# Reading the group and slot numbers for four visits at once in two edge sums of a GNN kernel

## The chip, the core and the metric

The kernel runs on one core of one Trainium2 chip. The metric is the device time in microseconds of one execution of the whole program.

## The reference, cut to what matters

The program computes four graph layers one after the other on one graph of 6,250 nodes and 100,000 edges, sorted by target node: two GAT convolutions, a GCN layer, a relational attention layer and a GGN (gated) layer, with a residual and a layer norm behind each. The change touches the edge sums of the GCN and of the GGN layer. What these must compute is a weighted and a plain sum of source rows by target node:

```
msgs = xw[row] * norm[:, None]                                   # GCN
out  = jax.ops.segment_sum(msgs, col, num_segments=n)
agg  = jax.ops.segment_sum(m[src], dst, num_segments=n_nodes)    # GGN
```

A row has 128 float32 numbers. Nodes are kept in 49 blocks of 128.

## The kernel before, in words

**Groups and visits.** The edges are cut into 196 groups (`GROUPS`) of 512 edges (`GE`), each as four tiles (`GT`) of 128 edges, one edge to a partition. A group touches one block of target nodes or, at a border, two or more. A pair of a group and a block is a visit; there are 244 (`V`). A visit multiplies, for each of the four tiles, a one-hot matrix (edge against node of the block, 128x128) with the gathered rows (128x128) on TensorE and adds the four products up in PSUM. Which group, which block and which buffer slot a visit has is only known at run time; an earlier stage writes these numbers into rows in SBUF (`grp_row`, `blk_row`, `slot_row`), and `done_row` says for each group which visit is its last.

**Who does what, in both stages.** All loops are written out in the program; nothing branches.

- POOL (`gather_rows`, L256) gathers the rows of each group with four indirect DMAs into one of 14 slots (`SLOTS`). From the fifteenth group on it first reads `done_row` (L956) and waits on `s_used`, which is the counter `s_o` of TensorE's finished visits, until the last visit of the group that held the slot is done.
- SP (`announce`, L965) waits for the four gathers of a group and adds one to `s_landed`.
- DVE makes the one-hot of the next visit (`front`, four operations, L1864 or L2051; two buffers), waits for TensorE's finished visit `s_o`, and adds the PSUM result to the accumulator (`back`, L1872 or L2059). It counts `s_oh` and `s_acc`.
- TensorE, per visit: it reads the group number (`group_of`, L975) and the slot number (`slot_of`, L978) from SBUF into registers, waits for the one-hot (`s_oh`), for the group's rows (`s_landed`) and for the accumulation of the visit two back (`s_acc`), and issues four float32 matmuls (L1946 in GGN, L2116 in GCN), whose last adds one to `s_o`. In the trace one such matmul is two weight loads and two matmul records.
- In the GCN stage TensorE has a second job after each of the first 208 visits (`static`, L2127): four small bf16 matmuls that pick node values for a later layer. It reads the four block numbers for it in one instruction (`several`, L969). ACT and DVE serve this job too (L2015, L2071, L2072), and ACT stores the one-hots it made to memory.

**Order.** Each engine runs its own program in order and meets the others only at semaphores. POOL may be up to 14 groups ahead of the last finished visit. A visit's number reads stand in TensorE's program behind the matmuls of the visit before.

**Around it.** The GCN stage begins with POOL's and TensorE's first instruction together. In the GGN stage POOL gathers its first 14 groups while TensorE and ACT do another job (13 rounds of four transposes and two matmuls, L1923 to L1936); visits start after it. What follows each stage waits for all of it.

Of the kernel before, what the change touches and what calls it, by code (L numbers as in the profile page):

```python
# [32 lines left out]
D = 128  # L33
# [9 lines left out]
V = GROUPS + BLOCKS - 1  # L43
# [7 lines left out]
RING = 4  # L51
# [37 lines left out]
def build(nc, A, out):  # L89
    top = ExitStack()  # L90
    with top:
# [885 lines left out]
        def slot_of(eng, v):  # L977
            return eng.value_load(slot_row[0:1, bass.ds(v, 1)], min_val=0, max_val=SLOTS - 1)  # L978

# [846 lines left out]
        def ggn_edges():  # L1826

            with phase() as st:
# [18 lines left out]
                with nc.Block() as block:  # L1847
# [69 lines left out]
                    def _(pe):  # L1917
# [19 lines left out]
                        for i in range(0, V // RING):  # L1937
                            for k in range(RING):
                                v = i * RING + k
                                g = group_of(pe, v)  # L1940
                                slot = slot_of(pe, v)
                                pe.wait_ge(s_oh, v + 1)
                                pe.wait_ge(s_landed, g + 1)
                                pe.wait_ge(s_acc, v + 1)
                                for t in range(GT):
                                    m = nc.tensor.matmul(ps_o[k % 2][:, 0:D], oh[:, k % 2, t, :], rows[:, bass.ds(slot, 1), t, :].rearrange("p o d -> p (o d)"),  # L1946
                                                         start=(t == 0), stop=(t == GT - 1))
                                m.then_inc(s_o, 1)


        def gcn_edges():
            with phase() as st:
# [33 lines left out]
                with nc.Block() as block:  # L1986
# [117 lines left out]
                    def _(pe):  # L2104
# [4 lines left out]
                        def body(n, k):  # L2109
                            g = group_of(pe, n)  # L2110
                            slot = slot_of(pe, n)
                            pe.wait_ge(s_oh, n + 1)
                            pe.wait_ge(s_landed, g + 1)
                            pe.wait_ge(s_acc, n + 1)
                            for t in range(GT):
                                m = mm(ps_o[k % 2][:, 0:D], oh[:, k % 2, t, :], rows[:, bass.ds(slot, 1), t, :].rearrange("p o d -> p (o d)"),  # L2116
                                       start=(t == 0), stop=(t == GT - 1))
# [13 lines left out]
                        for k in range(RING):  # L2131
                            body(k, k)
                            static(0, k)
                        for i in range(1, ITERS // RING):
                            for k in range(RING):
                                body(i * RING + k, k)
                                static(i, k)
                        for n in range(ITERS, V):
                            body(n, n % RING)
# [658 lines left out]
```

## Time and profile before

| what | us |
|---|---|
| median of 3 executions (lowest, highest) | 7929.77 (7909.9, 7938.46) |
| span of the profiled execution (the page gives no time of its own for it) | 7961.8 |
| GCN edge stage, first to last visit | 3380 to 4611 |
| GGN edge stage, first to last visit | 6761 to 7861 |
| PE busy, share of the span | 3988.6, 50% |
| DVE busy | 3552.5, 45% |
| POOL busy | 4190.2, 53% |

PE is TensorE's array, PEld its weight loads, PEldq and the other names with q an engine's own instruction queue: reads of numbers, register arithmetic and waits, which don't count as busy. In a row of the timeline the last bracket is the idle time of the engine before the row and what ended it; "issue" is time in which the engine waited for nothing that the profile shows. A releaser is inferred, and can be named after a line that is long over. The clock column is the granted TensorE clock as a share of full speed: 0.5 is 1.2 GHz, 1.0 is 2.4 GHz.

### The profile page before, as it was taken

The page shows a single profiled execution, that of the slowest core. Times are in us where ns is not written, and L with a number is a line of the kernel's source. Part 1 is how long each engine was busy: PE and PEld are TensorE (multiplying, and loading weights), DVE is VectorE, ACT ScalarE, POOL GpSimd, SP SyncE. Part 2 cuts the span into 40 slices and gives each one's busy share as a digit, 9 for nine tenths or more (in the row PEclk, how much of TensorE's full clock was granted, in tenths as well). Part 3 has the DMA queues.
Part 4 walks back from the last instruction along what each step waited for, and adds up shares of the span by engine and source line. Part 5 has one row for each costly group of instructions (what it writes and reads, how often), then busy time and mean ns, then how long its engine had stood idle before and what let it go on. Part 6 is the DMA issues. An engine that isn't in the chain of part 4 may idle for free. (4 is left out here: it accounts for less than half of the span.)

```text
span 7961.8 us, 106930 instructions
## 1 busy us (share of the span) xinstructions
PE 3988.6 (50%) x29332; PEld 3225.4 (41%) x29332; DVE 3552.5 (45%) x10985; ACT 1543.9 (19%) x3920; POOL 4190.2 (53%) x4416
## 2 busy tenths in 40 slices
PE   2401645540164442334444458888888585333446
PEld 1301534530154432323444446666666473233334
DVE  3002965530297442423333355555555693122224
ACT  0001730010174000200000033444344213000003
POOL 6474035537503566466665635555555644666662
PEclk8655557775555766655555578888888797566568
DMA  5233445643344554345666424445444372111111
GB/s 147 75 105 96 146 125 171 188 117 106 94 145 131 161 168 140 108 104 141 149 150 147 109 87 143 147 149 149 145 147 145 79 206 64 46 46 45 45 45 32
DMA packets 564740, 944.43 MB, mean 119 GB/s; under 512 B 122022, under 2 KB 226111, under 8 KB 563599
## 3 DMA queue, kind: packets, MB, share of 16 engines
q1 hardware_dynamic: 263779, 403.40, 15.9%
q0 software_dynamic: 140576, 316.92, 15.5%
q10 hardware_dynamic: 159840, 217.27, 9.7%
q8 instruction: 290, 4.75, 0.3%
q14 instruction: 255, 2.09, 0.1%
HBM read 703.64 MB, written 235.53 MB: 118 GB/s over the span
## 5 line engine op out<-in xcount | busy, mean ns | idle before, releaser
L256 POOL DMA_INDIRECT s_rows<-rel_tab,src_v x832 | 813.4, 978 | 700.0 <-DVE s_msg L2489 424.7
L256 POOL DMA_INDIRECT stash<-gat_tab,src_g x784 | 790.9, 1009 | 724.5 <-POOLq L111 383.2
L256 POOL DMA_INDIRECT stash<-in_x,src_g x736 | 740.4, 1006 | 719.3 <-POOLq L111 382.6
L1163 PE MATMUL g_psc<-g_parts,g_oh 128*128 128x52 bf16 x9408 | 507.0, 220 | 1060.3 <-issue 796.5
L256 POOL DMA_INDIRECT gcn_rows<-gcn_tab,src_g x784 | 753.0, 960 | 461.8 <-issue 222.4
L256 POOL DMA_INDIRECT ggn_rows<-ggn_tab,src_g x784 | 744.2, 949 | 423.0 <-issue 231.0
L1600 PE MATMUL e_psb<-tmp,e_oh 128*128 x3328 | 565.5, 334 | 751.4 <-DVE e_oh L1571 470.4
L1163 PEld LDWEIGHTS g_psc<-g_parts,g_oh 128*128 128x128 bf16 x9408 | 439.7, 120 | 1128.2 <-issue 843.8
L1600 PEld LDWEIGHTS e_psb<-tmp,e_oh 128*128 128x128 f32 x3328 | 510.5, 237 | 806.7 <-issue 806.5
L1946 PE MATMUL ggn_pso<-ggn_rows,ggn_oh 128*128 x1952 | 448.7, 390 | 652.3 <-issue 277.2
L2116 PE MATMUL gcn_pso<-gcn_rows,gcn_oh 128*128 x1952 | 503.3, 433 | 531.4 <-issue 387.1
L1946 PEld LDWEIGHTS ggn_pso<-ggn_rows,ggn_oh 128*128 128x128 f32 x1952 | 371.1, 277 | 730.5 <-issue 729.8
L2116 PEld LDWEIGHTS gcn_pso<-gcn_rows,gcn_oh 128*128 128x128 f32 x1952 | 425.0, 317 | 566.2 <-issue 564.8
L1095 DVE TENSOR_TENSOR g_eq<-g_eq,g_psc 128x416 f32<-128x416 f32 x392 | 227.6, 581 | 832.3 <-remote 572.0
L1055 ACT ACTIVATE acc<-g_lo_rows,g_neg_pid 128x512 f32<-128x512 bf16 x392 | 283.0, 722 | 1008.7 <-issue 776.1
L1872 DVE TENSOR_TENSOR acc<-acc,ggn_pso 128x128 f32 x244 | 69.8, 286 | 915.7 <-DMA edge_v<-acc 626.2
L2059 DVE TENSOR_TENSOR acc<-acc,gcn_pso 128x128 f32 x244 | 69.8, 286 | 784.1 <-remote 517.2
L1569 DVE COPY tmp<-gx 128x12 f32<-128x12 f32 x392 | 75.7, 193 | 680.5 <-DMA edge_v<-stash 288.4
L2558 PE MATMUL s_psk<-w_kv,s_msgT 128*128 128x128 f32 x1664 | 301.0, 336 | 0.0
L1571 DVE TENSOR_TENSOR e_oh<-iota,drel_v 128x512 f32<-128x512 f32 x416 | 284.3, 683 | 21.7 <-PE e_psb L1600 21.7
L2563 PE MATMUL s_psv<-w_kv,s_msgT 128*128 128x128 f32 x1664 | 280.8, 325 | 0.2
L2558 PEld LDWEIGHTS s_psk<-w_kv,s_msgT 128*128 128x128 f32 x1664 | 254.2, 234 | 58.1 <-issue 58.1
(503 smaller groups left out, 8232.0 us busy)
## 6 DMA issues: line engine op xcount, KB each, us to landing
edge_v<-stash SPq DMA_DIRECT2D x392, 256.0 KB, 2.1
g_lo_rows<-lo_rows ACTq DMA_DIRECT2D x392, 256.0 KB
e_values<-edge_v SPq DMA_DIRECT2D x392, 256.0 KB
oh_dram<-tmp ACTq DMA_DIRECT2D x208, 256.0 KB
s_oh<-oh_dram SPq DMA_DIRECT2D x208, 256.0 KB
edge_v<-acc SPq DMA_DIRECT2D x208, 256.0 KB
r_values<-edge_v SPq DMA_DIRECT2D x208, 256.0 KB, 3.0
tmp<-drel_rows ACTq DMA_DIRECT2D x208, 128.0 KB
```

The lines of the kernel that those rows point to most:

```text
L256: pool.indirect_dma_start(rows[:, t, :], None, tab[:, :], bass.IndirectOffsetOnAxis(ap=edges[:, t:t + 1], axis=0)).then_inc(s_land, 16)
L1055: nc.scalar.activation(sq[:, k % 2, :], trow[:, k, GE:2 * GE], ACT.Square, bias=neg_pid[:, :]).then_inc(s_sq, 1)
L1095: v.tensor_tensor(eq[:, k % 2, :, :, :], eq[:, k % 2, :, :, :], cand, ALU.mult).then_inc(s_take, 1)
L1163: m = nc.tensor.matmul(ps_c[k % 2][:, a * GT + t, 0:NBP], oh[:, k, a * GE + t * P:a * GE + (t + 1) * P], part[:, a, n, :], start=(n == 0), ...
L1569: v.tensor_copy(wv4[:, k, :, D:WCOLS], w.rearrange("p h t -> p t h"))
L1571: v.tensor_tensor(oh[:, k % RING, :, :], iota[:, :].unsqueeze(1).to_broadcast([P, GT, P]), drel_v[:, bass.ds(n * GT, GT)].unsqueeze(2).to_ ...
L1600: nc.tensor.matmul(ps_b[:, bass.ds(bank, 1), 0:WCOLS].rearrange("p o d -> p (o d)"), oh[:, k, t, :], wv[:, bass.ds(slot, 1), :].rearrange( ...
L1872: v_.tensor_tensor(ab, ab, ps_o[k % 2][:, 0:D], ALU.add).then_inc(s_acc, 1)
L1946: m = nc.tensor.matmul(ps_o[k % 2][:, 0:D], oh[:, k % 2, t, :], rows[:, bass.ds(slot, 1), t, :].rearrange("p o d -> p (o d)"), start=(t == ...
L2116: m = mm(ps_o[k % 2][:, 0:D], oh[:, k % 2, t, :], rows[:, bass.ds(slot, 1), t, :].rearrange("p o d -> p (o d)"), start=(t == 0), stop=(t = ...
L2558: m = mm(ps_k[:, t, :], msgT[:, T[t]], w_kv[:, 0, :], start=False, stop=(t == GT - 1))
L2563: m = mm(ps_v[:, t, :], msgT[:, T[t]], w_kv[:, 1, :], start=True, stop=True)
```

## The change

TensorE no longer reads two numbers for each visit. At the first of every four visits (`RING` is 4) it reads the group number of the fourth of them, reads the four slot numbers with one instruction, and waits until the rows of the fourth visit's group have landed. The three visits behind it have no number reads and no wait on `s_landed`. The waits on `s_oh` and `s_acc`, the matmuls and all other engines' programs stay as they were. In GCN the second job stays between the visits; its loop is rewritten so that the visits 208 to 243 run through the same code.

```diff
-                                g = group_of(pe, v)
-                                slot = slot_of(pe, v)
+                                if k == 0:
+                                    newest = group_of(pe, v + RING - 1)
+                                    slots = several(mybir.EngineType.PE, slot_row[0:1, bass.ds(v, RING)], SLOTS - 1)
+                                    pe.wait_ge(s_landed, newest + 1)
                                 pe.wait_ge(s_oh, v + 1)
-                                pe.wait_ge(s_landed, g + 1)
                                 pe.wait_ge(s_acc, v + 1)
                                 for t in range(GT):
-                                    m = nc.tensor.matmul(ps_o[k % 2][:, 0:D], oh[:, k % 2, t, :], rows[:, bass.ds(slot, 1), t, :].rearrange("p o d -> p (o d)"),
+                                    m = nc.tensor.matmul(ps_o[k % 2][:, 0:D], oh[:, k % 2, t, :], rows[:, bass.ds(slots[k], 1), t, :].rearrange("p o d -> p (o d)"),
                                                          start=(t == 0), stop=(t == GT - 1))
                                 m.then_inc(s_o, 1)
...
-                        def body(n, k):
-                            g = group_of(pe, n)
-                            slot = slot_of(pe, n)
+                        def numbers(n):
+                            newest = group_of(pe, n + RING - 1)
+                            slots = several(mybir.EngineType.PE, slot_row[0:1, bass.ds(n, RING)], SLOTS - 1)
+                            pe.wait_ge(s_landed, newest + 1)
+                            return slots
+
+                        def body(n, k, slots):
                             pe.wait_ge(s_oh, n + 1)
-                            pe.wait_ge(s_landed, g + 1)
                             pe.wait_ge(s_acc, n + 1)
...
-                        for k in range(RING):
-                            body(k, k)
-                            static(0, k)
-                        for i in range(1, ITERS // RING):
+                        for i in range(0, V // RING):
+                            slots = numbers(i * RING)
                             for k in range(RING):
-                                body(i * RING + k, k)
-                                static(i, k)
-                        for n in range(ITERS, V):
-                            body(n, n % RING)
+                                body(i * RING + k, k, slots)
+                                if i < ITERS // RING:
+                                    static(i, k)
```

`several`, which both versions have, reads a row of numbers into as many registers with one instruction.

## Rows read from the trace of the kernel before

**Rows 1.** Stretches of both stages: us, busy by engine (count), clock, DMA share, GB/s.

```profile
3380.00:4611.00 1231.00, 553.90 (x2784) 485.33 (x2784) 447.72 (x1642) 39.74 (x210) 745.57 (x777) 0.52 0.52 130
4578.00:4611.00 33.00, 24.00 (x128) 20.66 (x128) 20.01 (x77) 0.00 (x0) 0.00 (x0) 0.80 0.00 1
6761.00:7861.00 1100.00, 448.31 (x1952) 370.93 (x1952) 269.26 (x1224) 0.04 (x1) 691.30 (x728) 0.62 0.17 44
7829.00:7861.00 32.00, 23.11 (x129) 19.82 (x128) 16.46 (x76) 0.00 (x0) 0.00 (x0) 0.82 0.00 1
```

**Rows 2.** Groups of the GCN stage: busy us, mean ns | idle before, releasers.

```profile
L256 POOL DMA_INDIRECT gcn_rows<-gcn_tab,src_g x777 | 745.6, 960 | 449.4 <-issue 220.5 <-remote 115.5 <-PE gcn_pso L2116 113.4
L2116 PE MATMUL gcn_pso<-gcn_rows,gcn_oh 128*128 x1952 | 503.3, 433 | 531.4 <-issue 387.1 <-DVE acc L2059 97.5 <-DVE gcn_oh L2051 25.1
```

**Rows 3.** The same groups of the GGN stage.

```profile
L256 POOL DMA_INDIRECT ggn_rows<-ggn_tab,src_g x728 | 691.3, 950 | 396.5 <-issue 204.5 <-DMA edge_v<-acc 145.4 <-PE ggn_pso L1946 46.6
L1946 PE MATMUL ggn_pso<-ggn_rows,ggn_oh 128*128 x1952 | 448.7, 390 | 652.3 <-issue 277.2 <-DVE acc L1872 262.8 <-DVE ggn_oh L1864 103.8
L1872 DVE TENSOR_TENSOR acc<-acc,ggn_pso 128x128 f32 x243 | 69.5, 286 | 914.0 <-DMA edge_v<-acc 626.2 <-PE ggn_pso L1946 228.6 <-issue 59.1
```

**Rows 4.** Timeline after the last gather, GGN: start us, us, what [idle before, releaser].

```profile
7835.52 0.97 PEld L1946 LDWEIGHTS ggn_pso<-ggn_rows,ggn_oh 128*128 128x128 f32 x8 [0.85 <-issue]
7835.52 1.15 PE L1946 MATMUL ggn_pso<-ggn_rows,ggn_oh 128*128 x8 [0.67 <-DVE acc L1872]
7836.89 0.29 DVE L1872 TENSOR_TENSOR acc<-acc,ggn_pso 128x128 f32 x1 [0.75 <-PE ggn_pso L1946]
7837.10 0.87 DVE L1864 TENSOR_SCALAR ggn_oh<-iota,dst_tab 128x128 f32<-128x128 f32 x4
7837.55 0.97 PEld L1946 LDWEIGHTS ggn_pso<-ggn_rows,ggn_oh 128*128 128x128 f32 x8 [1.07 <-issue]
```

**Rows 5.** Timeline after the last gather, GCN, weight loads at half clock.

```profile
4578.69 1.78 PEld L2116 LDWEIGHTS gcn_pso<-gcn_rows,gcn_oh 128*128 128x128 f32 x8 [1.07 <-issue]
4580.72 1.78 PEld L2116 LDWEIGHTS gcn_pso<-gcn_rows,gcn_oh 128*128 128x128 f32 x8 [0.24 <-issue]
```

**Rows 6.** Slot read L978 after the last gather: ns min/median/max.

```profile
L978 PEldq TENSOR_LOAD <-slot_row x15: 299/300/307, 7830.5 to 7859.1; - x15
L978 PEldq FUSED_REGOPS  x16: 151/151/151, 7828.9 to 7859.5; - x16
L978 PEldq SEQ_ASSERT  x16: 18/18/18, 7829.1 to 7859.7; - x16
```

**Rows 7.** Slot read L978 at 6770.5 to 6784 us, gathers running.

```profile
L978 PEldq FUSED_REGOPS  x2: 697/703/709, 6772.0 to 6782.5; - x2
```

**Rows 8.** Four-number read in the GCN stage.

```profile
L969 PEldq TENSOR_LOAD <-blkv_row x208: 5/342/934, 3380.4 to 4502.9; - x104
```

**Rows 9.** Timeline of the first waits of POOL and one round, GGN.

```profile
6762.85 0.94 POOL L256 DMA_INDIRECT ggn_rows<-ggn_tab,src_g  x1 [24.54 <-PE ggn_pso L1946]
6791.81 0.94 POOL L256 DMA_INDIRECT ggn_rows<-ggn_tab,src_g  x1 [3.10 <-DMA edge_v<-acc]
6796.74 0.97 PEld L1946 LDWEIGHTS ggn_pso<-ggn_rows,ggn_oh 128*128 128x128 f32 x8 [0.33 <-issue]
6806.13 0.29 DVE L1872 TENSOR_TENSOR acc<-acc,ggn_pso 128x128 f32 x1 [8.24 <-DMA edge_v<-acc]
6820.57 0.29 DVE L1872 TENSOR_TENSOR acc<-acc,ggn_pso 128x128 f32 x1 [13.38 <-DMA edge_v<-acc]
6820.75 0.94 POOL L256 DMA_INDIRECT ggn_rows<-ggn_tab,src_g  x1 [4.20 <-DMA edge_v<-acc]
```

**Rows 10.** Stretches of the GGN opening, with gathers and without.

```profile
6694.00:6737.00 43.00, 9.61 (x16) 3.53 (x15) 0.00 (x0) 3.94 (x6) 32.64 (x35) 0.50 0.20 54
6750.00:6759.00 9.00, 9.00 (x29) 4.71 (x27) 0.00 (x0) 6.93 (x11) 0.00 (x0) 0.89 0.01 2
```

**Rows 11.** Landing announcements L965, GCN.

```profile
L965 SPq EVENT_SEMAPHORE  x195: 17/17/17, 3384.2 to 4577.9; - x195
```

More of the change, by code:

```diff
@@ L975, in group_of @@
             return eng.value_load(grp_row[0:1, bass.ds(v, 1)], min_val=0, max_val=GROUPS - 1)
-        def slot_of(eng, v):
-            return eng.value_load(slot_row[0:1, bass.ds(v, 1)], min_val=0, max_val=SLOTS - 1)
         def landed(name, slots=SLOTS):
@@ L2107, in _ @@
                         pe.sem_inc(s_acc, 2)
-                        def body(n, k):
-                            g = group_of(pe, n)
-                            slot = slot_of(pe, n)
+                        def numbers(n):
[4 more added lines that the diff above has]
+                        def body(n, k, slots):
                             pe.wait_ge(s_oh, n + 1)
-                            pe.wait_ge(s_landed, g + 1)
                             pe.wait_ge(s_acc, n + 1)
                             for t in range(GT):
-                                m = mm(ps_o[k % 2][:, 0:D], oh[:, k % 2, t, :], rows[:, bass.ds(slot, 1), t, :].rearrange("p o d -> p (o d)"),
+                                m = mm(ps_o[k % 2][:, 0:D], oh[:, k % 2, t, :], rows[:, bass.ds(slots[k], 1), t, :].rearrange("p o d -> p (o d)"),
                                        start=(t == 0), stop=(t == GT - 1))
```

## The prediction

> **What bounds the kernel now.** I first took the busy times by stretch, for the two stages that the change touches. GCN takes 1231 us and GGN 1100 us [rows 1]. In neither is an engine full: PE's array is busy for 554 and 448 us, DVE for 448 and 269, POOL for 746 and 691. The groups of instructions say more. POOL's gathers take 0.96 and 0.95 us each, and between two of them stand some 0.3 us of "issue", which no other engine causes: 745.6 + 220.5 = 966 us in GCN and 691.3 + 204.5 = 896 us in GGN [rows 2, 3]. The remainder of POOL's idle time is waiting, 115.5 + 113.4 = 229 us in GCN, and 145.4 + 46.6 = 192 us in GGN, of which 24.5 us is the first wait, before any visit is done [rows 2, 3, 9]. The rest, 229 + 167.5 = 396 us, are waits for a slot, so for finished visits of TensorE. After the last landing each stage still runs for 33 and 32 us [rows 1, 11]: some 16 visits that TensorE is behind. So the path through a stage is POOL's gathers, its waits for TensorE, and the visits left over at the end.
>
> Why is TensorE behind? With the gathers over, a visit takes 2.03 us from start to start, and it takes the same 2.03 us whether its eight weight loads take 0.97 us (full clock) or 1.78 us (half clock) [rows 4, 5]. The array is not what bounds it, and DVE's 0.29 + 0.87 us isn't either [rows 4]. What is left is the queue of instructions: a number read is 0.30 us of load, 0.15 us of clamp and 0.02 us of assertion [rows 6], with gaps some 0.65 us, and there are two in a row for each visit. At 2.03 us, 244 visits would need 495 us, under half of either stage, and TensorE would never be behind. But while the gathers run it falls into another gait. In the round of [rows 9] POOL resumes at 6791.81; the visit that starts at 6796.74 should end 1.15 us later, as in [rows 4], and DVE takes its result only at 6806.13, where 0.22 us after the end is the rule with the gathers over. The next result is taken at 6820.57, and then POOL resumes after a wait of 4.2 us. At the same time single instructions of TensorE's queue, which take 0.15 us undisturbed, take 0.7 us [rows 6, 7]. So TensorE's reports of finished work arrive late while POOL gathers, its queue crawls, and POOL runs out of slots because of it. DVE's idle 626 us in GGN is the same thing seen from DVE (the releaser's name there is a line long over) [rows 3].
>
> **What the change removes.** Per four visits, eight reads of three queue instructions each become one such read and one four-number read, which the same engine does in 0.34 us in the GCN stage [rows 8]: 8 x 0.65 = 5.2 us of queue time become 0.65 + 0.40 = 1.05 us. Counted in instructions, a GGN visit has 12 in the queue (two reads of three, two waits or sums, four address computations) and 16 array instructions, 28 in all. Afterwards it has 5 and a quarter of 6, so 6.5, and 22.5 in all. With the second job a GCN visit goes from 47 to 41.5. Nothing is moved on SP, POOL, ACT or DVE, and no DMA is touched.
>
> *The end of each stage.* Here it counts in full. Without the reads the queue needs 2.03 - 1.3 + 0.26 = 1.0 us for a visit, and the next bound takes over: over two visits, a visit's matmuls 1.15, the way to DVE 0.22, 0.21 until its one-hots start and 0.87 for them, then TensorE again [rows 4], (1.15 + 0.22 + 0.21 + 0.87)/2 = 1.2 us and a little for issue, at full clock; 1.8 us at half clock by the weight loads [rows 5]. The clock is 0.8 there [rows 1], and I take 1.6 us. 16 visits x 0.43 = 7 us in each stage, **14 us** (bounds: 4 us if all ran at half clock, 2 x 16 x 0.8 = 26 us at full clock).
>
> *POOL's waits.* How much of the 396 us goes depends on what makes the reports late, which no row shows. The least is nothing, if the queue's instructions have no part in it. The most by this count is that the waits vanish. In between: if the late reports are a backlog to which each instruction of TensorE adds alike, a round carries more visits in the proportion of the counts, and the waits shrink by 5.5/28 = 20% in GGN and 5.5/47 = 12% in GCN: 33 + 27 = **60 us**. I take this value. It is near the lower end, since most of what TensorE does, the array's 16 or 24 instructions, stays.
>
> *The new wait.* Behind it stand the block's four visits, and with them DVE's additions, ACT's copies and POOL's slots. As long as TensorE is some 14 groups behind POOL, the fourth visit's rows have long landed and it costs nothing. At the head of the GCN stage they have not: a group lands every 5 us (four gathers of 1.25), the second at 3384.2 [rows 11], so the fourth at about 3394, and the first visit starts 14 us later. POOL has slots until its fifteenth group, 70 us in, so only part of it comes through: between 0 and 14 us, I take **3 us**. In GGN all 14 groups are there before the first visit.
>
> **The sum.** -14 - 60 + 3 = -71 us. The durations are from an execution with a span of 7961.8 us, 32 us or 0.4% above the median; the difference is put on the median: 7929.8 - 71 = **7859 us**.
>
> The Trainium skill, in "NOTIFIC — the notification-queue block", section on the write path and its measured rates, says that an instruction's own record costs an engine no cycles, though the block's inner queue can hold its producers back when it is full. By the first half the reads that are gone never cost more than their 0.65 us, and the sum would be 7929.8 - 14 + 3 = 7919 us. The trace speaks against it: 0.7 us for an instruction of 0.15 us [rows 6, 7]; no row shows that it is records which are held back.
>
> **The rivals.**
>
> *The waits stay* (7919 us, no change). The backlog comes from the array's instructions alone. For it: in the opening of the GGN stage TensorE's program has no number reads and hardly any waits, and yet with the gathers running PE is busy for 9.6 of 43 us, against 9.0 of 9.0 us once they pause [rows 10]. The late reports need no number reads. Then only the stage ends gain: 7929.8 - 14 + 3 = 7919.
>
> *The crawl goes by the queue.* In it each of a visit's queue steps costs 0.7 us [rows 7], 12 and four matmuls today, 6.5 and four afterwards. The visits in a crawl would come in 10.5/16 of the time, and about half of GGN's and a quarter of GCN's waits would go: 84 + 57 + 14 - 3 = 152 us, 7778 us. Against it: DVE waits for a report, not for a queue, in the long gaps of [rows 9].
>
> *The crawl is gone altogether.* It came from number reads and gathers together. All 396 us go, and TensorE follows POOL so closely that only the last four visits are left after the last landing, 6 instead of 33 us twice: 7929.8 - 396 - 53 = 7481 us. Against it stand again [rows 10].
>
> *Slower: denser visits fill the backlog sooner.* If what TensorE may leave unreported is used up in a fixed time or by the rate of its matmuls, then visits at 1.4 to 1.8 us after each resumption of POOL, instead of 2.03, start the crawl earlier, and their four-visit heads, which wait for both reads and rows, fall into it. Of about five visits that a GGN round carries (from 6791.81 to the wait before 6820.75 are 24.7 us, 20 gathers, so five groups), half a one would be lost, so 10% more rounds and waits: +40 us. With the whole 14 us at the head of GCN and the end's gain: 40 + 14 - 14 = +40 us, 7970 us. It decides from the point where a round carries fewer than the present visits. For it: POOL resumes at 6791.81 and the visit of 6796.74, five microseconds on, is already late [rows 9].
>
> That the change does not do what it says is not likely: the four-number read is in use in the same stage [rows 8].
>
> **How the numbers follow.** A measurement of this kernel can tell about 0.5%, or 40 us, from no change. The forecast has 0.40, on its own from 7810 to 7900; most of it is beyond 40 us. The waits that stay have 0.24, the queue's crawl 0.17, its end 0.08, the slower case 0.11. Faster by over 0.5%: 0.38 + 0.17 + 0.08 + a little of the second case, 0.65. Within 0.5%: 0.26. Slower: 0.09, as the slower case lies at its border. The range goes from 7740 to 7960: below it lies the vanished crawl, above it half of the slower case.
>
> **What would show each step.** (1) After the last gather, visits in both stages at 1.3 to 1.8 us instead of 2.03; if they stay at 2.03, the queue was not the bound. (2) POOL's waits, without the first: 134 us in GGN and 202 us in GCN; 168 and 229 if the array alone makes the backlog, near nothing if the crawl is gone. (3) Undisturbed reads of the group number 61 times in each stage, the four-number read of the slots 61 times at about 0.34 us. (4) The first GCN visit at about 3394 instead of 3380. (5) All other stages as before. The forecast is wrong if POOL's waits grow, or if they fall by more than half.

## The result

The changed kernel takes 7866.8 us (median of 20 runs; the kernel before beside it 7934.1 us, of 20 runs). The ratio is 0.9928 with a 95% interval of 0.9909 to 0.9947, so 57 us less (42 to 72). The medians differ by 67 us: three of the changed kernel's 20 runs had a granted clock of 0.56 to 0.58 instead of 0.67 and took 7949 to 7963 us, and the ratio leaves out only the longest of them, as a slow run. A later measurement gave 0.9934 (0.9912 to 0.9955). The prediction was 7859 us, between 7740 and 7960: the direction and the size are right. On one chip, though (chip B below), where both kernels run in 6000 us, the same change made the kernel slower by 0.25%. The experiments below show what is missing on that chip, and most likely why the change costs time there.

### The profile page after: what moved, and what is told of

The parts are those of the page before. It is cut to its first block and busy times, and to the rows that moved or that the text cites. A ratio compares the mean times of both kernels' runs of the same rounds, so it can differ in the third digit from the quotient of the medians.

```text
span 7853.1 us, 104124 instructions
## 1 busy us (share of the span) xinstructions
PE 3880.8 (49%) x29332; PEld 3174.1 (40%) x29332; DVE 3549.2 (45%) x10985; ACT 1546.6 (20%) x3920; POOL 4220.9 (54%) x4416
## 3 DMA queue, kind: packets, MB, share of 16 engines
q8 instruction: 279, 4.57, 0.2%
## 5 line engine op out<-in xcount | busy, mean ns | idle before, releaser
L256 POOL DMA_INDIRECT s_rows<-rel_tab,src_v x832 | 818.7, 984 | 685.7 <-DVE s_msg L2487 411.6
L256 POOL DMA_INDIRECT gcn_rows<-gcn_tab,src_g x784 | 756.7, 965 | 418.2 <-issue 225.8
L256 POOL DMA_INDIRECT ggn_rows<-ggn_tab,src_g x784 | 746.7, 952 | 411.6 <-issue 234.3
L1597 PE MATMUL e_psb<-tmp,e_oh 128*128 x3328 | 584.8, 341 | 708.2 <-DVE e_oh L1568 379.8
L1597 PEld LDWEIGHTS e_psb<-tmp,e_oh 128*128 128x128 f32 x3328 | 527.9, 244 | 765.4 <-issue 765.0
L1944 PE MATMUL ggn_pso<-ggn_rows,ggn_oh 128*128 x1952 | 381.6, 368 | 704.4 <-DVE ggn_oh L1861 302.4
L1944 PEld LDWEIGHTS ggn_pso<-ggn_rows,ggn_oh 128*128 128x128 f32 x1952 | 344.4, 269 | 742.3 <-issue 740.5
L2117 PE MATMUL gcn_pso<-gcn_rows,gcn_oh 128*128 x1952 | 444.5, 402 | 159.7 <-issue 118.3
L2117 PEld LDWEIGHTS gcn_pso<-gcn_rows,gcn_oh 128*128 128x128 f32 x1952 | 387.4, 295 | 178.2 <-issue 173.2
L2128 PE MATMUL pre_psr<-vt_nv_pieces,tmp 128*128 x832 | 92.9, 181 | 526.5 <-DVE tmp L2070 348.7
L2128 PEld LDWEIGHTS pre_psr<-vt_nv_pieces,tmp 128*128 128x128 bf16 x832 | 81.2, 113 | 565.9 <-issue 551.3
```

Of the source, the lines that this page charges most:

```text
L256: pool.indirect_dma_start(rows[:, t, :], None, tab[:, :], bass.IndirectOffsetOnAxis(ap=edges[:, t:t + 1], axis=0)).then_inc(s_land, 16)
L1597: nc.tensor.matmul(ps_b[:, bass.ds(bank, 1), 0:WCOLS].rearrange("p o d -> p (o d)"), oh[:, k, t, :], wv[:, bass.ds(slot, 1), :].rearrange( ...
L2128: m = mm(ps_n[k % 2][:, t, :], oh2[:, k, t * P:(t + 1) * P], nvp[:, bass.ds(b, 1), :].rearrange("p o n -> p (o n)"), start=True, stop=True)
```

## The profile after

The stretches of both stages and their ends, to be read against [rows 1] (us, then busy time and count of PE, weight loads, DVE, ACT and POOL; granted clock, DMA share, GB/s):

```profile
3343.00:4534.00 1191.00, 511.09 (x2784) 453.34 (x2784) 446.37 (x1657) 39.96 (x210) 756.72 (x784) 0.58 0.52 136
4508.00:4534.00 26.00, 20.60 (x139) 17.70 (x138) 21.12 (x84) 0.00 (x0) 0.67 (x1) 0.95 0.06 6
6575.00:7753.00 1178.00, 423.11 (x2051) 362.75 (x2049) 276.68 (x1234) 24.71 (x39) 746.32 (x784) 0.62 0.17 44
7724.00:7753.00 29.00, 21.55 (x144) 19.81 (x144) 19.32 (x92) 0.00 (x0) 0.42 (x1) 0.85 0.04 6
```

These windows reach from the first gather to the last addition, those of [rows 1] from the first visit. Measured from first gather to last addition in both traces, GCN went from 1240.5 to 1190.9 us and GGN from 1192.9 to 1178.2: 49.6 and 14.7 us, 64 in all. The two profiled spans differ by 109 us (7961.8 and 7853.1). The other 45 us lie in stages that the change doesn't touch: the span before is 28 us above the median of 7934.1, the span after 14 us below its own.

POOL, DVE and PE in the two stages, against [rows 2, 3] (busy us, mean ns | idle us before, releasers):

```profile
L256 POOL DMA_INDIRECT gcn_rows<-gcn_tab,src_g x784 | 756.7, 965 | 418.2 <-issue 225.8 <-remote 157.9 <-PE gcn_pso L2117 25.2
...
L2117 PE MATMUL gcn_pso<-gcn_rows,gcn_oh 128*128 x1952 | 444.5, 402 | 159.7 <-issue 118.3 <-DVE gcn_oh L2049 22.3 <-DVE acc L2057 12.4
...
L256 POOL DMA_INDIRECT ggn_rows<-ggn_tab,src_g x784 | 746.7, 952 | 411.6 <-issue 234.3 <-DMA edge_v<-acc 133.6 <-PE ggn_pso L1944 43.6
...
L1869 DVE TENSOR_TENSOR acc<-acc,ggn_pso 128x128 f32 x244 | 70.0, 287 | 901.1 <-DMA edge_v<-acc 667.0 <-PE ggn_pso L1944 208.8 <-issue 25.0
...
L1944 PE MATMUL ggn_pso<-ggn_rows,ggn_oh 128*128 x1952 | 381.6, 368 | 704.4 <-DVE ggn_oh L1861 302.4 <-issue 277.4 <-DVE acc L1869 123.9
```

A gather still takes 0.95 to 0.97 us and its issue 0.3 us. What is left of POOL's idle time is waiting for slots: 418.2 - 225.8 = 192 us in GCN, where it was 229, and 411.6 - 234.3 - 24.3 (the first wait) = 153 us in GGN, where it was 167.5. DVE's idle time before its additions in GGN is 901 us where [rows 3] has 914 (the row after also includes the first addition, which in the trace before adds under 2 us), so the late reports are nearly all still there.

After the last gather, two visits of GGN and the start of the next two, against [rows 4] (start us, us, what [idle before, releaser]):

```profile
7737.06 2.12 PE L1944 MATMUL ggn_pso<-ggn_rows,ggn_oh 128*128 x16 [0.58 <-DVE acc L1869]
7738.51 0.29 DVE L1869 TENSOR_TENSOR acc<-acc,ggn_pso 128x128 f32 x1 [0.73 <-PE ggn_pso L1944]
7738.71 0.87 DVE L1861 TENSOR_SCALAR ggn_oh<-iota,dst_tab 128x128 f32<-128x128 f32 x4
7739.49 0.28 DVE L1869 TENSOR_TENSOR acc<-acc,ggn_pso 128x128 f32 x1
...
7739.72 2.13 PE L1944 MATMUL ggn_pso<-ggn_rows,ggn_oh 128*128 x16 [0.54 <-DVE ggn_oh L1861]
```

Two visits now take 7739.72 - 7737.06 = 2.66 us, 1.33 each, and TensorE waits for one-hots and additions and no longer for its queue.

A round of GGN with the gathers running, against [rows 9]: POOL's resumption, DVE's additions, POOL's next resumption:

```profile
6772.57 0.95 POOL L256 DMA_INDIRECT ggn_rows<-ggn_tab,src_g  x1 [4.69 <-DMA edge_v<-acc]
...
6781.23 0.29 DVE L1869 TENSOR_TENSOR acc<-acc,ggn_pso 128x128 f32 x1 [2.90 <-PE ggn_pso L1944]
...
6794.64 0.29 DVE L1869 TENSOR_TENSOR acc<-acc,ggn_pso 128x128 f32 x1 [12.21 <-DMA edge_v<-acc]
...
6806.55 0.29 DVE L1869 TENSOR_TENSOR acc<-acc,ggn_pso 128x128 f32 x1 [10.84 <-DMA edge_v<-acc]
...
6807.12 0.94 POOL L256 DMA_INDIRECT ggn_rows<-ggn_tab,src_g  x1 [4.73 <-DMA edge_v<-acc]
```

The long gaps are still there. But from 6772.57 to the wait before 6807.12 are 29.8 us, 24 gathers, six groups, where the round of [rows 9] has five. These are single rounds. Over the whole GGN stage, from one gap between gathers of over 3 us to the next, POOL now gathers 5.9 groups in the mean instead of 5.1; the gaps of over 1 us are 48 instead of 53, and about as long as before (3.4 for 3.3 us in the mean).

The reads in GGN: the group numbers now come 61 times, the four slots in one load:

```profile
L975 PEldq TENSOR_LOAD <-grp_row x61: 302/305/314, 6665.4 to 7746.5; - x61
...
L969 PEldq TENSOR_LOAD <-slot_row x61: 328/332/334, 6666.1 to 7747.1; - x61
```

No load is slowed here, gathers or not. The clamps show the same. Before, of the slot number with the gathers running (ns min/median/max), then after, of the group number over the whole stage:

```profile
L978 PEldq FUSED_REGOPS  x227: 2/151/715, 6762.3 to 7825.2; - x114
...
L975 PEldq FUSED_REGOPS  x61: 151/151/157, 6665.8 to 7746.8; - x61
```

With the gathers running, 296 of 1815 steps of register arithmetic and assertion in TensorE's GGN queue took over 0.5 us before the change, and none of 1015 does after it; in GCN it was 228 of 2645 and is 19 of 1854. The slow queue that [rows 7] shows is gone from GGN and nearly gone from GCN. The reports are no earlier for it: from a visit's last matmul to DVE's addition it took 2.9 us in the mean in GCN and 5.2 us in GGN, and it takes 5.3 and 5.9 us now.

## The experiments

In what follows a *pause* is a gap of over 1 us between two gathers, less the 0.3 us of issue; a *report's delay* is the time from a visit's last matmul to DVE's addition. Both are worked out from the events of a trace. Four of the runs fell on one chip (A), four on a second (B), four on a third (C); the changed kernel ran again on B and C. The chip of the first measurement, that of the result and of the profiles before and after, isn't on record. The kernel before was profiled only there, so its pauses and stages are known only from it. The edits are shortened; those of "the wait without the reads" and "each read twice" are against the kernel before, the others against the changed kernel.

**The reads without the wait.** Four group numbers are read at once too, and each visit waits for its own group:

```diff
-newest = group_of(pe, v + RING - 1)
+groups = several_checked(PE, grp_row[0:1, bass.ds(v, RING)], GROUPS - 1)
 slots = several(PE, slot_row[0:1, bass.ds(v, RING)], SLOTS - 1)
-pe.wait_ge(s_landed, newest + 1)
 pe.wait_ge(s_oh, v + 1)
+pe.wait_ge(s_landed, groups[k] + 1)
```

> The changed kernel, but TensorE also reads the four group numbers at once, and each visit waits for the rows of its own group, as before the change. So it has the fewer reads without the new wait. Compare with the changed kernel (7866.8 us; POOL's waits of over 1 us: 165.1 us in GCN, 162.7 in GGN; a visit every 1.49 and 1.42 us after the last gather; first GCN visit 21.8 us after the first gather). If the gain is the reads' alone (my theory): first GCN visit back to some 9.5 us after the first gather, all else as in the changed kernel, time 7855 to 7870 us. If the wait at the head of four was what helped (it lets a backlog drain, a rival): POOL's waits back towards 210 and 174 us, time 7900 us or more.

Measured on A: 8007.4 us beside 8041.2 of the kernel before, ratio 0.9956 (0.9938 to 0.9973). The first GCN visit is back at 10.8 us after the first gather. But pauses are 189 and 182 us, and the ratio isn't that of the changed kernel. Its checked read brings instructions of its own: it has 1708 fewer than the kernel before, 3.5 for each of the 488 visits, where the change has 5.75 fewer. So a gain is there without the wait, 35 us of it. That the rest is missing because fewer instructions are saved is an argument; this run alone would also allow the wait a share, which the next one has to tell.

**The wait without the reads.** Both reads of each visit stay; the first of four reads the fourth's group and waits for it, the other three don't wait for rows:

```diff
-g = group_of(pe, v)
+g = group_of(pe, v + RING - 1 if k == 0 else v)
 slot = slot_of(pe, v)
 pe.wait_ge(s_oh, v + 1)
-pe.wait_ge(s_landed, g + 1)
+if k == 0:
+    pe.wait_ge(s_landed, g + 1)
```

> The kernel before with its two reads for each visit, but the first visit of four reads the group number of the fourth and waits for it, and the other three wait for no rows. The new wait alone. If it costs only at the head of GCN (my theory): first GCN visit some 22 us after the first gather instead of 9.5, POOL's waits as before (210 and 174 us of pauses over 1 us, within 15), visits after the last gather 2.06 us, time 0 to 14 us over the kernel before. If the wait is part of the gain (rival): POOL's waits fall by over 20 us and the time is 7900 us or less. If it costs in every block of four: POOL's waits grow by over 20 us.

Measured on A: 8033.6 us, ratio 0.9989 (0.9976 to 1.0001), pauses 201 and 180 us, first GCN visit at 22.2 us. Its pauses and its visits at the stage ends (1.97 us) are about those of the profile before (210 and 174, 2.06). The new wait is not the gain (9 us at most likely, between -1 and 19) nor, on this chip, a loss that can be seen.

**Each read twice.** Six queue instructions more for each visit than before the change:

```diff
+group_of(pe, v)
+slot_of(pe, v)
 g = group_of(pe, v)
 slot = slot_of(pe, v)
```

> The kernel before with each of the two number reads of a visit done twice: 6 instructions more in TensorE's queue per visit, the change the other way round. If every TensorE instruction adds alike to the backlog (my forecast's term): POOL's waits grow by 6/28 in GGN and 6/47 in GCN (+37 and +27 us), and the visits after the last gather go from 2.06 to some 3.3 us (+40 us in both stages): 8030 us. If only the array's instructions make the backlog: waits as before, only the visits at the stage ends slower: about 7970 us. If the crawl goes by queue instructions at 0.7 us each: 6 x 0.7 us more for every visit that runs in it, waits grow by 38% (+145 us): 8120 us or more.

Measured on A: 8362.1 us, ratio 1.0408 (1.0384 to 1.0433), 321 us more than the kernel before (328 by the ratio). The rows of POOL:

```profile
L256 POOL DMA_INDIRECT gcn_rows<-gcn_tab,src_g x784 | 756.8, 965 | 635.6 <-PE gcn_pso L2120 393.1 <-issue 213.1 <-remote 19.0
...
L256 POOL DMA_INDIRECT ggn_rows<-ggn_tab,src_g x784 | 744.4, 950 | 535.1 <-PE ggn_pso L1948 260.6 <-issue 231.5 <-DMA edge_v<-acc 43.0
```

Against the profile before, which is of the first measurement, pauses rise to 378 and 285 us, by 278 in all, and the stage ends by 52 (a visit takes 3.35 us there). The forecast's own term, each instruction alike, expected 64 us of pauses and missed by over four times; "only the array" is out too. The third expectation, 8120 us or more with 145 us of pauses, was open upwards and is the only one that the time doesn't exclude, but its pauses were too few by half. A likely reason is the slack: with the gathers running a group lands every 5 us and there are 1.24 visits for each, so TensorE has 4.0 us a visit, and 3.35 us of queue without any disturbance leave it little with which to catch up. No run tests that.

**Half the array instructions.** One-hots in bf16, and of each gathered value only the upper 16 bits; the sums leave out the lower ones:

```diff
-oh = sb(st, "gcn_oh", [P, 2, GT, P])
+oh = sb(st, "gcn_oh", [P, 2, GT, P], BF16)
+rows_16 = <rows seen as bf16, halves h = 0, 1>
-mm(ps_o[k % 2][:, 0:D], oh[:, k % 2, t, :], rows[:, bass.ds(slots[k], 1), t, :], ...)
+mm(ps_o[k % 2][:, 0:D], oh[:, k % 2, t, :], rows_16[:, bass.ds(slots[k], 1), t, :, 1:2], ...)
```

> The changed kernel, with the one-hots of both stages in bf16 and, of each gathered value, the upper 16 bits read as bf16: one pass of TensorE instead of two or more, so 8 array instructions in place of 16 in each visit's sum; the sums leave out the lower 16 bits of the values. Queue instructions and the waits are those of the changed kernel. If every TensorE instruction adds alike (forecast's term): POOL's waits fall by 8/22.5 in GGN and 8/41.5 in GCN (162.7 to 114, 165.1 to 133 us), the visits at the stage ends go from 1.45 to about 1.1 us: 7866 - 49 - 32 - 12 = 7775 us. If the backlog is made by the queue's instructions alone: waits as in the changed kernel, only the stage ends gain, 7855 us. If it is a matter of time and not of counts: waits as in the changed kernel too, and the crawl sets in 3.5 to 4.3 us after POOL resumes as now, whatever the number of instructions in that time.

Measured on A: 7929.7 us, ratio 0.9856 (0.9837 to 0.9875), so 0.72% below the changed kernel's ratio, 58 us. Pauses are 161 and 151 us (the profile after: 165 and 163). The direction is the forecast's, the size two thirds of it (58 of 91 us), and less of it appears as pauses than expected: 4 and 12 us, not 32 and 49. The changed kernel did not run on A, and the other three of A have GGN pauses of about 180 us and more, so part of the difference is the chip's. Against the kernel with its own rows, which ran on A too and has 10.25 instructions more a visit, it is 78 us faster and its pauses are 28 and 31 us shorter. The edit takes away more than a count: TensorE's array is busy for 522 us in the two stages, where the changed kernel on C has 946, at a granted clock of 0.50 and 0.51 for 0.59 and 0.61. And the clamps of its queue are slow again, up to 1.4 us, though its queue has the changed kernel's instructions.

**Changed kernel on chip B.**

> The changed kernel again, unaltered, beside the following ones on one chip, so that their stages can be compared with its own. Expected: a ratio of 0.9928 within 0.002 to the kernel before, POOL's pauses of over 1 us at 165 and 163 us within 10. If the separate-row kernel's 0.9956 and its 189 and 182 us were the chip's and not the reads', this one shows them too.

Measured: 6012.4 us beside 5998.2 of the kernel before, ratio 1.0025 (1.0014 to 1.0035). Its POOL rows:

```profile
L256 POOL DMA_INDIRECT gcn_rows<-gcn_tab,src_g x784 | 751.4, 958 | 248.2 <-issue 235.5 <-POOLq L111 9.3 <-PE gcn_pso L2117 3.4
...
L256 POOL DMA_INDIRECT ggn_rows<-ggn_tab,src_g x784 | 745.1, 950 | 249.1 <-issue 242.7 <-PE ggn_pso L1944 6.4
```

A gather takes what it takes elsewhere, but there is not one pause. The reports' mean delay is 0.31 and 0.23 us in the two stages, none is over 1.1 us, where the profile after has 5.3 and 5.9 us, and 152 and 132 of 244 over 2 us. The same program has late reports on one chip and none on another, so they need something of the chip (or of what it is set up with). Without them TensorE follows the gathers, and the reads that the change removes lie in time in which it waits for rows. GGN's announcements (ns min/median/max, first and last start), and then the timeline of the stage's end:

```profile
L965 SPq EVENT_SEMAPHORE  x196: 17/17/17, 4928.7 to 5909.2; - x196
```

```profile
5909.36 4.65 PE L1944 MATMUL ggn_pso<-ggn_rows,ggn_oh 128*128 x24 [9.75 <-SPq L965]
...
5914.32 1.15 PE L1944 MATMUL ggn_pso<-ggn_rows,ggn_oh 128*128 x8 [0.31 <-DVE ggn_oh L1861]
5915.69 0.29 DVE L1869 TENSOR_TENSOR acc<-acc,ggn_pso 128x128 f32 x1 [1.18 <-PE ggn_pso L1944]
```

The last group is announced at 5909.2. Only then do the last four visits begin, all four, since their head waits for it; TensorE had been idle for 9.75 us. They end 6.5 us later, in GCN 7.2. Three of them, at some 1.75 us each, could have been done before. That is an estimate of 5 us in each stage, 10 of the 15 us by which the kernel is slower. Where the other 5 are isn't shown. Nor is the 10 measured: the kernel before has no profile from B, and the kernel that takes this wait back (below) did not run there.

**Plain transfers in place of gathers.** In GGN ScalarE loads whole blocks of 128 rows, other rows than the graph's, and POOL does nothing:

```diff
-gather_rows(pool, rows, ggn_tab, s_row, s_o)
...
+for g in range(GROUPS):
+    ...  (ScalarE waits for the slot as POOL did)
+    for t in range(GT):
+        act.dma_start(rows[:, k, t, :], ggn_tab[r * P:(r + 1) * P, :]).then_inc(s_row[k], 16)
```

> The changed kernel, but in the GGN stage ScalarE loads the rows with plain transfers of whole blocks of 128 rows, in place of POOL's indirect gathers (other rows than the graph's, the same bytes into the same slots, the same waits for free slots). TensorE's program is unaltered. If POOL's gathers are what makes TensorE's reports late: DVE takes each visit's result some 0.2 us after its end all through the stage, no FUSED_REGOPS takes 0.7 us, visits run at 1.3 to 1.8 us and the stage ends in 350 to 600 us instead of 1178: 7300 to 7050 us in all. If it is TensorE's own number of instructions, or the rows' traffic, whoever starts it: late reports of over 5 us remain, and the stage takes over 900 us.

It fell on B, where there were no late reports to cure: 5538.9 us, ratio 0.9237 (0.9221 to 0.9254), visits from 4949.7 to 5436 us. The stage is shorter there (486 us, with the gathers 994) because POOL's gathers, one every 1.25 us, no longer set its length. Whether they make reports late it could not say, so it was repeated on C:

> Rows of the GGN stage by ScalarE's plain transfers instead of POOL's indirect gathers, once more, as the first time fell on a chip without late reports. On a chip with them: if POOL's gathers are what makes TensorE's reports late, the stage runs as it did there (about 500 us in all, DVE takes a result within 0.3 us of its end). If TensorE's own instructions or the rows' traffic make them late: reports over 5 us late in this stage too, and over 700 us for it.

Measured on C: 7229.1 us, ratio 0.910 (0.906 to 0.914). First this kernel's GGN stage and its row of DVE's additions, then the stage of the changed kernel, both on C (columns as in the stretches and groups above):

```profile
6645.00:7131.00 486.00, 316.50 (x1952) 292.75 (x1952) 263.01 (x1225) 0.00 (x0) 0.00 (x0) 0.84 0.37 105
```

```profile
L1868 DVE TENSOR_TENSOR acc<-acc,ggn_pso 128x128 f32 x244 | 69.8, 286 | 255.2 <-PE ggn_pso L1951 252.7 <-issue 1.6
```

```profile
6736.00:7821.00 1085.00, 394.91 (x1954) 357.57 (x1952) 269.14 (x1225) 0.86 (x2) 691.87 (x728) 0.61 0.17 45
```

TensorE's program is the same, instruction for instruction. The bytes per us more than doubled (105 against 45 GB/s). And the reports are on time: mean delay 0.25 us, the longest 0.7, none over 2, against 5.8 us and 133 in the changed kernel beside it. In the GCN stage of the very same execution, where POOL still gathers, the mean is 5.2 us. The stage takes 486 us on C as it does on B. So on a chip that has late reports POOL's gathers are needed for them, and neither the bytes nor TensorE's program alone makes them. Whether it is POOL as the issuer or the indirect transfers isn't told apart, as the edit changed both.

**Deeper rings.** Four one-hot buffers and four PSUM banks instead of two, TensorE up to three visits ahead of the additions:

```diff
-oh = sb(st, f"ggn_oh", [P, 2, GT, P])
+oh = sb(st, f"ggn_oh", [P, RING, GT, P])
-front(v + 1, k + 1)
+front(v + RING - 1, (k + RING - 1) % RING)
-pe.wait_ge(s_acc, v + 1)
+pe.wait_ge(s_acc, max(v - 1, 2))
```

> The changed kernel with four one-hot buffers and four PSUM banks in place of two in both stages: DVE builds one-hots three visits ahead, TensorE may start a visit before the reports of the three before it are taken. Same instructions. If late reports hold the visits up (in GGN a visit starts when DVE has taken a late report and built the next one-hot): POOL's pauses in GGN fall from 163 to under 90 us and the time by 60 us or more; GCN, where TensorE's queue itself crawls, falls less. If only the queue's pace counts: pauses in both stages as in the changed kernel within 15 us, gain at the stage ends alone (1.4 to 1.2 us a visit, 7 us in all), time within 15 us of it.

Measured on B: 6012.2 us, ratio 1.0029 (1.0017 to 1.0040), the changed kernel's time. There are no pauses on B that it could shorten, so it says nothing of its question, and it had no second run. Whether late reports hold visits up through the two buffers stays open.

**No numbers at all.** Slots, groups and POOL's wait values are constants of an evenly spread order of visits, not the graph's:

```diff
-newest = group_of(pe, v + RING - 1)
-slots = several(PE, slot_row[0:1, bass.ds(v, RING)], SLOTS - 1)
+newest = (v + RING - 1) * GROUPS // V
+slots = [(v + j) * GROUPS // V % SLOTS for j in range(RING)]
```

> The changed kernel with no numbers read in the two stages: slot, group and POOL's wait values are constants of an evenly spread order of visits (244 visits over 196 groups), not the graph's. TensorE's queue has no reads and no address computations for the visits: about 2.25 queue instructions a visit in GGN instead of 6.5. Array instructions, one-hots, gathers as in the changed kernel. From the four kernels measured so far the time falls by about 10 us for each queue instruction a visit that is taken away (5.75 give 57 us, 3.5 give 35, 0.75 give 9), so here by 45 us against the changed kernel, ratio to before 0.987, POOL's pauses some 20 us less in each stage. If what is left of the late reports comes from the array's instructions: no change beyond 10 us. If the crawl has a threshold that a thin queue stays under: pauses near nothing, 250 us less.

On B: 6009.4 us, ratio 1.0018 (1.0009 to 1.0027). All reads gone, nothing gained: there the queue never was on the path. Repeated on C:

> No number reads and no address computations for the visits (slots, groups and POOL's wait values constant), once more for the same reason. On a chip with late reports: by 10 us for each queue instruction a visit, 45 us less than the changed kernel, POOL's pauses some 20 us less in each stage; no change if the array's instructions make the rest; 250 us less if a thin queue escapes the late reports. On one without: the changed kernel's time within 5 us, since TensorE waits for rows in either.

Measured on C: 7849.2 us, ratio 0.988 (0.985 to 0.991), 44 us less than the changed kernel beside it (7893.4), where 45 were expected. But pauses are 157 and 157 us, 14 and 6 less where 20 each were expected, and the two stages together are 25 us shorter in the traces. The two medians' difference has an interval of some 30 us to either side, so the hit owes something to luck. POOL's number reads are gone too in this kernel, and the order of visits is another; their shares aren't told apart. Its POOL rows:

```profile
L256 POOL DMA_INDIRECT gcn_rows<-gcn_tab,src_g x784 | 750.3, 957 | 413.3 <-issue 218.0 <-remote 173.2 <-PE gcn_pso L2117 13.0
...
L256 POOL DMA_INDIRECT ggn_rows<-ggn_tab,src_g x784 | 744.7, 950 | 404.0 <-issue 223.3 <-DMA edge_v<-acc 142.1 <-PE ggn_pso L1944 30.3
```

**Own rows at both ends.** The changed kernel, but in the first and last four visits of a stage each waits for its own group:

```diff
+own = i in (0, V // RING - 1)
-newest = group_of(pe, v + RING - 1)
+if k == 0 or own:
+    newest = group_of(pe, v if own else v + RING - 1)
+    pe.wait_ge(s_landed, newest + 1)
```

> The changed kernel, but in the first and the last four visits of each stage every visit waits for its own group, as before the change; the slots are still read four at once. On the chip of the last four runs POOL never waited for TensorE in either stage, the changed kernel was 0.25% slower, and after the last landing four visits were left, 7.2 and 6.5 us, as the head of the last four had waited for the last group. On such a chip this kernel should take back 8 to 12 us: ratio 0.999 to 1.001. On a chip whose reports come late, as in the runs before those, TensorE is 16 visits behind at the end, and only the head of GCN is won: the changed kernel's time or up to 12 us less.

Measured on C: 7884.4 us, ratio 0.9928 (0.9900 to 0.9955), beside the changed kernel's

> The changed kernel unaltered, to compare the others with on this chip. If TensorE's reports come late here (POOL pauses of over 1 us sum to more than 100 us a stage): ratio 0.990 to 0.995. If not (no pauses): ratio 1.002 to 1.004. Anything else speaks against the account that the gain is the late reports' alone.

7893.4 us, ratio 0.9934 (0.9912 to 0.9955), with pauses of 171 and 163 us. The first GCN visit is 9.7 us after the first gather instead of 22.1, and the stage is 2.3 us shorter (1189.8 against 1192.1). The two can't be told apart here. On a chip like B, for which it was made, it did not run.

**Time by instructions taken from TensorE.** Differences to the kernel before, by the ratios; the counts are those of each trace, divided by the 488 visits of both stages:

| kernel, chip | instructions less per visit | us less (95%) | us per instruction |
|---|---|---|---|
| wait alone, A | 0.75 | 9 (-1 to 19) | 12 |
| reads alone, A | 3.5 | 35 (22 to 50) | 10.1 |
| the change, first measurement | 5.75 | 57 (42 to 72) | 9.9 |
| the change, C | 5.75 | 52 (36 to 70) | 9.1 |
| no numbers, C | 11.0 | 95 (72 to 119) | 8.7 |
| the change and half the array, A | 13.75 | 116 (101 to 131) | 8.4 |
| each read twice, A | -6 | -328 (-348 to -309) | 55 |

By these times an instruction that a visit does without is worth 8 to 12 us, so some 17 to 25 ns for one instruction of one visit. But the intervals are wide, and the rows come from different chips. The length of the two stages in the traces, first gather to last addition, is steadier: 2369 and 2367 us for the changed kernel in two measurements.

| from, to | instructions less per visit | stages us, from and to | us per instruction |
|---|---|---|---|
| each read twice, wait alone (A) | 6.75 | 2776, 2439 | 50 |
| before, the change (first measurement) | 5.75 | 2433, 2369 | 11.2 |
| wait alone, reads alone (A) | 2.75 | 2439, 2407 | 11.4 |
| reads alone, half the array (A) | 10.25 | 2407, 2346 | 6.0 |
| the change, no numbers (C) | 5.25 | 2367, 2343 | 4.7 |

There is one trace of each, but the order is plain: the price of an instruction falls as the program gets thinner, from 50 us over 11 to about 5. It isn't one price for all. The step that is mostly array instructions (6.0) and the one of queue instructions alone (4.7) lie close together. The three instructions of an undisturbed read take 0.65 us with their gaps, 0.22 us each, where 11 us over 488 visits are 0.023 us.

## Why the prediction held

*What bounds the stage: POOL's gathers, its waits, the visits left over.* Right wherever reports were late. Stage lengths fell by 64 us in the profiles. Pauses gave 56 (210 to 165 in GCN, 174 to 163 in GGN) and the ends after the last gather 18 (36.3 to 25.3 and 35.4 to 28.4 us); the gathers themselves, at 965 for 960 and 952 for 949 ns, cost 6 us more and the short gaps between them 4.

*The ends, -14 us, 2.03 to 1.6 us a visit.* Measured 18 us, 2.06 to 1.49 and 1.42. The mechanism is that of sign 1; the size was a little low. The granted clock in the tail was higher than assumed (0.95 and 0.85 against 0.80 and 0.82 in [rows 1]), which goes with it but isn't all: GCN, with the higher clock, has the slower visits. The lower bound of the prediction, 4 us, is of one stage; for both, as its upper bound is, it is 2 x 16 x 0.23 = 7 us.

*POOL's waits, -60 us.* By the rows that the forecast used, 229 went to 192 and 167.5 to 153: 51 us less. The sum was near, the split wasn't: -27 and -33 were forecast for GCN and GGN, -37 and -14.5 came. Chip C repeats it (171 and 163 us of pauses). That the sum came close is in part luck: one stage gave more than the model said, the other less than half. In GGN the count promised 28/22.5, so 1.24 times as many groups from one long gap to the next, and they became 1.15 times as many (5.9 for 5.1). Why GCN gains more no run shows; when each read was doubled its pauses also grew more than GGN's, by 167 against 111 us.

*Its queue crawls, and POOL runs out of slots because of it.* This step took the slow queue and the late reports for one thing, and the profile after separates them. The slow queue steps went, all 296 in GGN and 209 of 228 in GCN, and only 51 of the 396 us of waits went with them; the reports in GCN even became later, from 2.9 to 5.3 us in the mean. So the slowness of the reads in the queue is not what POOL mainly waits for; the late reports are, and what makes them late stays open.

*Every TensorE instruction adds alike.* This was the choice between far bounds (0 and 396 us). In kind it fits: the step of mostly array instructions brought 6.0 us for each, that of queue instructions alone 4.7. In number it doesn't: the first ones were worth about 11 us each, the next ones about 5, and six more cost 50 each. So the model of equal shares is off, though its sum came near here. And the run that halves the array's instructions also shortens its work, so count and time aren't separated there. What stands behind it, which queue or buffer fills, no run shows. The fetching of instructions, which would also have one price for each, isn't enough by itself: the profile's DMA queue named instruction has 279 packets, 4.57 MB, for the changed kernel both in the first measurement and on B, and on B no report is late.

The Trainium skill, in "NOTIFIC — the notification-queue block", has both halves of a rule: by its section "Constraints, capacities, measured rates" an instruction's record costs the engine nothing, and by its section "The write path" the block's inner pipeline holds its producers back rather than lose a record. The prediction took the first half to mean that the reads are worth nothing beyond the stage ends; in the first measurement and on A and C they were worth more, as 51 us of waits in the first. The second half could make instructions of every kind cost something, as they did; but no run took the records away, and B shows no late report, so it isn't shown that it is they.

*The new wait, +3 us.* It does what was said at the head of GCN (first visit 21.8 us after the first gather instead of 9.5), and of those 12 us next to nothing comes through: taking them back gave 2 us of stage on C. But the prediction looked only at the head. The wait also stands at the end of each stage, where it is free only because TensorE is 16 visits behind. On B it is not behind, and by the estimate above the wait costs some 5 us a stage. The text counted "only the last four visits" in its rival of a vanished crawl, and didn't notice that this is a price of the change.

*The rivals.* "The waits stay" (7919) is out where reports are late: 51 us of the waits went; it is in effect what B does. "The crawl goes by the queue" (7778) expected 141 us of the waits: out. "Gone altogether" (7481) is out by its time, though the slow queue steps that it starts from did go; the waits hardly followed. The slower case wanted fewer groups in a round, and there are more. B made the change slower, most likely by a mechanism that none of them had: without late reports there is nothing to win, and the wait is left. That a chip might have none was not considered, and the profile of one chip can't tell.

## What to carry to other kernels

Where an engine's reports come late, don't price what you remove by its undisturbed duration: here one instruction less a visit was worth about 23 ns at first and 10 ns later, though a read of three took 650 ns of queue. And don't take a slow queue for the cause of the waits beside it: here it went, and seven eighths of the waits stayed. A wait that is moved ahead for a block is free only while the engine lags behind what it waits for; look at both ends of the loop, and where the engine keeps up, try the fine waits in the first and the last block (no run shows their gain here). And before tuning against such a lag, see on a second chip whether it has it.

## What was not expected of the hardware

The same kernel takes 7934 us in the first measurement, 8041 on A, 7940 on C and 5998 on B, 24% less. In the changed kernel's two stages a gather takes 0.95 to 0.97 us in all its traces. The difference is in POOL's waiting, and not only there: in the five stages in which POOL gathers, the gaps of over 1 us between two gathers sum to 1857 us for the changed kernel in the first measurement and to 43 us on B, and the two spans differ by 1837 us. In the two stages that the change touches, on B none of TensorE's reports takes over 1.1 us, while in the first measurement and on C their mean is over 5 us, the longest 56 and 55 us, in GCN. POOL's gathers are needed for it in GGN, as the plain transfers at over twice the rate show; what differs between the chips, no run can tell.

The kernel with each read doubled has few late reports (mean 0.6 and 1.1 us, against 2.9 and 5.2 before the change) and yet the longest pauses, and 239 and 256 slow steps in its queue; the changed kernel has hardly a slow step and the latest reports. So it seems that the same disturbance shows either in the queue's steps or in the reports, which no run tests by itself. A short delay of reports isn't by itself a sign that all is well.
